# Second expert layer of a fused two-layer kernel on one Trainium2 core: factors of eight tiles at once, roots on VectorE, gathers before scatters, four and two banks

## What is computed

```python
gates = softmax(hn @ router_w.T)             # 8 experts, each token takes the best K = 2
h_e = gelu(hn @ w1[e]) @ w2[e]               # 128 -> 256 -> 128, for both experts e of a token
x = x + gate_1 * h_1 + gate_2 * h_2
...
mu = jnp.mean(x, axis=-1, keepdims=True)
out = (x - mu) * jax.lax.rsqrt(var + 1e-5)
```

## Time and profile before

| | |
|---|---|
| three runs, us | 2051.05, 2042.49, 2050.25 |
| median, us | 2050.25 |
| the profiled execution, us | 2048.84 |
| its span, us | 2046.8 |
| TensorE busy, us | 1752.1 (86%) |
| VectorE busy, us | 1418.8 (69%) |
| ScalarE busy, us | 1357.5 (66%) |
| GpSimd busy, us | 1056.0 (52%) |
| mean granted TensorE clock | 0.940 of full speed |

### The profile page before, as it was taken

The page is one execution under the profiler, slowest core; times in us unless marked ns, Lnnn a source line. Parts: engine busy times, 40 slices in busy tenths (PEclk is TensorE's granted clock), DMA queues, the critical chain, the costliest instruction groups (busy, mean ns, idle before and its releaser), DMA issues. The chain is left out here.

```text
span 2046.8 us, 52138 instructions
## 1 busy us (share of the span) xinstructions
PE 1752.1 (86%) x15928; PEld 1417.6 (69%) x15928; DVE 1418.8 (69%) x5901; ACT 1357.5 (66%) x3347; POOL 1056.0 (52%) x1384
## 2 busy tenths in 40 slices
PE   7789999999999998898999579888859999559885
PEld 6555555555555566787999458777738999529884
DVE  2378787878887885584432279999749889586775
ACT  3488888888888873423455358888749898417774
POOL 2133333333333323116567578888438899816664
PEclk9799999999999997999999779999979999859998
DMA  7789999999999973105576412222131222267552
GB/s 229 266 287 308 319 304 319 315 308 317 310 311 317 301 261 125 42 1 157 169 191 203 115 29 58 60 61 60 40 80 37 53 47 43 53 102 229 171 172 74
DMA packets 222093, 350.12 MB, mean 171 GB/s; under 512 B 56928, under 2 KB 169568, under 8 KB 221312
## 3 DMA queue, kind: packets, MB, share of 16 engines
q1 hardware_dynamic: 187024, 305.34, 47.6%
q0 software_dynamic: 14144, 31.16, 6.3%
q10 hardware_dynamic: 20656, 10.29, 1.7%
HBM read 160.82 MB, written 144.67 MB: 149 GB/s over the span
## 5 line engine op out<-in xcount | busy, mean ns | idle before, releaser
L183 POOL TENSOR_SCALAR_AFFINE_SELECT heads_raw_relative<-heads_raw_relative 128x508 f32<-128x508 f32 x256 | 166.7, 675 | 499.7 <-ACT heads_raw_relative L568 461.0
L568 ACT COPY heads_raw_relative<-heads_rel_bank 128x768 f32<-128x768 f32 x247 | 198.7, 804 | 125.1 <-PE heads_rel_bank L463 125.1
L492 PE MATMUL attend_turn_bank<-ident,attend_score 128*128 128x128 f32 x1536 | 232.8, 288 | 20.5 <-ACT attend_prob_t L574 19.2
L492 PEld LDWEIGHTS attend_turn_bank<-ident,attend_score 128*128 128x128 f32 x1536 | 164.3, 142 | 117.9 <-ACT attend_prob_t L574 68.3
L574 ACT ACTIVATE attend_prob_t<-attend_turn_bank 128x384 f32<-128x384 f32 x512 | 224.8, 500 | 7.3 <-PE attend_turn_bank L492 7.3
L578 ACT ACTIVATE attend_score<-attend_score,attend_extreme 128x128 f32<-128x128 f32 x512 | 215.6, 421 | 9.1 <-DVE attend_extreme L625 8.8
L625 DVE CUSTOM_DVE_ANT_0 attend_score<-attend_score_bank,heads_relative 128x256 f32<-128x256 f32 x512 | 215.0, 420 | 0.0
L622 DVE CUSTOM_DVE_ANT_0 attend_score<-attend_score_bank,heads_relative 128x128 f32<-128x128 f32 x512 | 146.7, 287 | 78.2 <-PE attend_score_bank L463 52.2
L631 DVE TENSOR_SCALAR attend_score<-attend_score,attend_extreme 128x256 f32<-128x256 f32 x512 | 195.7, 382 | 0.0
L1422 POOL DMA_INDIRECT moe_route_rows_sb<-tokens,moe_taken x154 | 145.7, 946 | 70.4 <-PE moe_route_bank L1444 42.0
L463 PE MATMUL attend_score_bank<-heads_qk 32*128 32x256 f32 x1024 | 156.9, 383 | 0.0
(11 more groups left out here) (434 smaller groups left out, 5257.5 us busy)
## 6 DMA issues: line engine op xcount, KB each, us to landing
shear<-heads_raw_relative SPq DMA_DIRECT2D x128, 768.0 KB, 5.4
heads_relative<-shear SPq DMA_DIRECT2D x128, 768.0 KB, 5.6
duo_w_now<-moe_w SPq DMA_DIRECT2D x158, 129.0 KB
moe_route_w_now<-moe_w SPq DMA_DIRECT2D x154, 129.0 KB
expert_out<-moe_route_y ACTq DMA_DIRECT2D x38, 256.0 KB
qk_heads<-heads_qk_out SPq DMA_DIRECT2D x32, 256.0 KB, 3.9
heads_qk<-qk_heads SPq DMA_DIRECT2D x128, 64.0 KB
pair_rows<-groups SPq DMA_DIRECT2D x16, 260.0 KB, 8.6
```

The lines of the kernel that those rows point to most:

```text
L183: m = nc.gpsimd.affine_select(out=future, in_=future, compare_op=ALU.is_ge, fill=-BIG, base=1 - P, pattern=[[0, QUAD], [1, P - 1]], channe ...
L492: mm = nc.tensor.transpose(bank[:, j * P:(j + 1) * P], score[:, (h - LAG) % RING, j * P:(j + 1) * P], c.ident[:, :])
L568: nc.scalar.copy(raw[:, ring, 2 * half:2 * half + 2, :], r_bank[:, :, 0:W]).then_inc(rel_moved, 1)
```

## The change

- GpSimd issues all 64 gathers and then all 64 scatters.
- The factors of eight tiles for all 32 steps of the walk are computed at once: `find_places(n)` for tiles 8n to 8n + 7 (seven operations, at u mod 16 = 4) and `weigh(n, lo, hi)` (five operations of up to 8 x 32 columns, at u mod 16 = 9, the third of which waits for the gathers of its tiles). `add_output` takes its factor from that table, by the register of the tile. The first eight tiles are done in two pieces: 0 and 1 at the start, 2 to 7 behind `add_output(0)`.
- The root goes to VectorE: eleven operations on up to 8 columns, each waiting for the one before (a first guess from the bits of the number and three Newton steps), in the place of the reciprocal. ScalarE keeps the copies and Gelu.
- The first product runs three units ahead, with four banks; the second has two banks, so `output(u)` waits for `add_output(u - 2)`.
- Registers are loaded for 8 units at a time (`UNITS_LOADED`), before for 4 (`LOADED`).

```diff
-    S, RING, DEEP, LEAD, AHEAD = UNITS, 12, 4, 36, 2
+    S, RING, DEEP, AHEAD, LOAD = UNITS, 12, 4, 3, UNITS_LOADED
+    HIDS, YS = 4, 2
+    PORTION, KEEP_AFTER = 8, 5
...
+        passed, stepped, of_low, weight = (c.rows[:, :, 32 * k:32 * (k + 1)] for k in range(4))
+        weight_from = D - NWALK
...
-            for t in range(NT + LEAD):
-                if t < NT:
-                    gather(t)
-                if t >= LEAD:
-                    scatter(t - LEAD)
+            for t in range(NT):
+                gather(t)
+            for t in range(NT):
...
-                wait_past(pe, hid_ready, u - 2)
+                wait_past(pe, hid_ready, u - HIDS + 1)
...
-                wait_past(pe, added, u - 2)
+                wait_past(pe, added, u - YS + 1)
...
-            def root(k):
-                cols = slice(starts[k], ends[k])
-                act.wait_ge(eps_set, 1)
-                act.wait_ge(moments_done, ends[k])
-                nc.scalar.activation(std[:, cols], moments[:, cols, 1], ACT.Sqrt, bias=eps[:, 0:1]).then_inc(rooted, 1)
-
...
+            def find_places(n):
+                cols = slice(PORTION * n, PORTION * (n + 1))
+                nc.vector.tensor_tensor(passed[:, cols, 0:NEDGE], bcast(pairs.slot_no[:, cols], NEDGE), along(pairs.until[:, :], PORTION),
+                                        ALU.is_ge).then_inc(placed, 1)
+                dve.wait_ge(placed, 7 * n + 1)
+                nc.vector.tensor_tensor(stepped[:, cols, 0:NEDGE], passed[:, cols, 0:NEDGE], along(pairs.step_code[:, :], PORTION), ALU.mult
...
-            def weigh(u, tile):
-                gathered(dve, needed(u))
-                dve.wait_ge(placed, 7)
-                wait_past(dve, shared_out, u - DEEP + 1)
-                nc.vector.scalar_tensor_tensor(out=part[u % DEEP][:, :], in0=flat(place[:, bass.ds(tile, 1), :]),
-                                               scalar=pairs.place_no[:, u:u + 1], in1=flat(rows_sb[:, bass.ds(tile, 1), 2 * D:]),
-                                               op0=ALU.is_equal, op1=ALU.mult).then_inc(parted, 1)
-
-            def share_of(u):
-                dve.wait_ge(parted, u + 1)
-                wait_past(dve, added, u - DEEP + 1)
-                nc.vector.tensor_tensor(share[u % DEEP][:, :], part[u % DEEP][:, 0:1], part[u % DEEP][:, 1:2], ALU.add).then_inc(shared_out, 1)
+            def weigh(n, lo, hi):
+                done, cols, count = 5 * n, slice(lo, hi), hi - lo
+                walk = along(pairs.unit_no[:, 0:NWALK], count)
+                dve.wait_ge(placed, 7 * ((hi - 1) // PORTION + 1))
+                nc.vector.tensor_tensor(of_low[:, cols, :], walk, bcast(place[:, cols, 0], NWALK), ALU.is_equal).then_inc(weighed, 1)
+                nc.vector.tensor_tensor(weight[:, cols, :], walk, bcast(place[:, cols, 1], NWALK), ALU.is_equal).then_inc(weighed, 1)
+                for t in range(lo, hi):
+                    gathered(dve, t)
+                dve.wait_ge(weighed, done + 1)
+                nc.vector.tensor_tensor(of_low[:, cols, :], of_low[:, cols, :], bcast(rows_sb[:, cols, 2 * D], NWALK), ALU.mult
...
+                nc.vector.tensor_tensor(weight[:, cols, :], weight[:, cols, :], of_low[:, cols, :], ALU.add).then_inc(weighed, 1)
 
             def add_output(u, tile):
                 dve.wait_ge(y_made, u + 1)
-                dve.wait_ge(shared_out, u + 1)
+                dve.wait_ge(weighed, 5 * sum(needed(u) >= first for first in weighed_from))
                 wait_past(dve, added, u)
                 total = flat(rows_sb[:, bass.ds(tile, 1), D:2 * D])
-                nc.vector.scalar_tensor_tensor(out=total, in0=y_bank[u % 3][:, 0:D], scalar=share[u % DEEP][:, 0:1], in1=total,
+                factors = weights_flat[:, weight_from + u:weight_from + u + (D - 2) * (NT - 1) + 1:D - 2]
+                nc.vector.scalar_tensor_tensor(out=total, in0=y_bank[u % YS][:, 0:D], scalar=factors[:, bass.ds(tile, 1)], in1=total,
                                                op0=ALU.mult, op1=ALU.add).then_inc(added, 1)
...
-            def invert(k):
-                cols = slice(starts[k], ends[k])
-                dve.wait_ge(rooted, k + 1)
-                nc.vector.reciprocal(rstd[:, cols], std[:, cols]).then_inc(inverted, 1)
+            def root(k):
+                cols, wide = slice(starts[k], ends[k]), slice(0, ends[k] - starts[k])
+                done = 11 * k
+                dve.wait_ge(moments_done, ends[k])
+                nc.vector.tensor_scalar(shifted[:, wide], moments[:, cols, 1], LN_EPS, None, ALU.add).then_inc(root_did, 1)
+                dve.wait_ge(root_did, done + 1)
+                nc.vector.tensor_scalar(rstd[:, cols].bitcast(I32), shifted[:, wide].bitcast(I32), -0.5, float(0x5f3759df), ALU.mult, ALU.add
+                                        ).then_inc(root_did, 1)
+                for i in range(3):
+                    dve.wait_ge(root_did, done + 3 * i + 2)
+                    nc.vector.scalar_tensor_tensor(out=step[:, wide], in0=rstd[:, cols], scalar=-0.5, in1=rstd[:, cols],
+                                                   op0=ALU.mult, op1=ALU.mult).then_inc(root_did, 1)
+                    dve.wait_ge(root_did, done + 3 * i + 3)
+                    nc.vector.tensor_tensor(step[:, wide], step[:, wide], shifted[:, wide], ALU.mult).then_inc(root_did, 1)
+                    dve.wait_ge(root_did, done + 3 * i + 4)
+                    nc.vector.scalar_tensor_tensor(out=rstd[:, cols], in0=step[:, wide], scalar=1.5, in1=rstd[:, cols],
+                                                   op0=ALU.add, op1=ALU.mult).then_inc(root_did, 1)
...
+            weighed_from = [0, 2] + list(range(PORTION, NT, PORTION))
...
+                    keep_at.setdefault(min(finished(end - 1) + KEEP_AFTER + j, S + 1), []).append((t, k))
+            find_places(0)
+            weigh(0, 0, 2)
+            for u in range(S + 2):
                 if u < S:
-                    if u + 1 < S:
-                        share_of(u + 1)
-                    add_output(u, tiles[u // LOADED % 2][u % LOADED])
+                    if u % LOAD == 0:
+                        tiles = tiles_of(mybir.EngineType.DVE, u)
+                    add_output(u, tiles[u % LOAD])
+                if u == 0:
+                    weigh(1, 2, PORTION)
+                following = u // 16 + 1
+                if u % 16 == 4 and following < NT // PORTION:
+                    find_places(following)
+                if u % 16 == 9 and following < NT // PORTION:
+                    weigh(following + 1, PORTION * following, PORTION * (following + 1))
```

106 lines of the change are left out of this document (45 added, 61 removed).

## The result

| | before | after |
|---|---|---|
| median of four runs, us | 2048.45 | 2071.36 |
| lowest and highest, us | 2042.49, 2051.05 | 2065.01, 2074.03 |
| profiled execution, its span, us | 2048.84, 2046.8 | 2069.09, 2067.3 |
| mean granted clock | 0.940 | 0.947 |

The ratio is 1.0104, with a 95% interval of 1.008 to 1.0127: the change makes the kernel 23 us slower. The forecast was 2047 us, 2028 to 2060. The time lies above the range, on the side to which I gave 0.14, and by none of the mechanisms that I listed for it.

What follows compares the result with a forecast made beforehand. TensorE was taken to bound the first 48 units or so, later ones losing time to ScalarE's table loads. Terms -8.5 (periods), +3.0 (before unit 50), +1.9 (end), +1.6 (clock) sum to -2.0 from 2048.84: 2047 us, range 2028 to 2060.

Steps and rivals of the forecast that it cites:

- the side to which I gave 0.14: Whole kernel: slower than before by over 0.5%, at a chance of 0.14.
- The tail from unit 146: End of the run: the keep of tile 48 comes behind a root of 2.1 us, not a 0.17 us reciprocal: +1.9 us.
- the stall changed its owner: Burst periods: TensorE's stall moves from ScalarE to VectorE at about its old size, 19.0 against 19.15 us; chance 0.53.
- one fall of the clock: TensorE, idling in pieces of 1.0 to 1.7 us, drops to half clock once: +1.6 us, bounds 0 and 13.
- a slack of 0.8 us: Second product with two banks: add_output u-2 may be 0.8 us late; a heavy half makes TensorE 3.8 us late.
- The six bursts ahead of unit 50: Finds and weighs at units 4, 9, 20, 25, 36 and 41 each hold the adds: +3.8 us.
- Registers are now loaded once in 8 units: VectorE's factor work: L2012 had waited 16.5 us for 40 register loads, 0.41 us each.
- Two units without keep are less still, about 1.0.: VectorE's work for two units without keep takes about 1.0 us, against TensorE's 1.89 us.
- The light half: The eight of 16 units without keeps, root or bursts; TensorE is the bound there, so no lateness is made good.
- The first (bursts cost half): VectorE's bursts cost about half of what was counted, through overlap or light units: 2033 us, faster, chance 0.33.
- The second (the clock falls with every burst): TensorE's clock halves at every burst, 8 to 11 times 1.7 us: 2061 us, slower, chance 0.14.
- no gap under 2 us does: Ground against the clock falling with bursts: in the earlier trace no TensorE gap under 2 us preceded a fall.

Runs made afterwards that it cites:

- the shorter portion: The spread kernel with three banks and loads of four, its portion of tiles 48 to 55 cut in two: 2021.8 us (0.9891).
- the spread kernels: Changed kernel, find, weigh and first six roots issued one or two operations behind each add_output: 2021.7 us (three banks, loads of four), 2040.9 us (change's banks and loads).

## Why the prediction was wrong

**What held.** Durations: the root spans 2.27 us (2.1), the find from 1913.18 to the operation behind it 2.15 (2.1), the weigh 1.8 (1.9). ScalarE's table waits left TensorE. Gathers ahead cost nothing. The tail from unit 146 grew by 2.4 us (+1.9), and the root makes most of it: back on ScalarE it leaves 32.0 us. By the shorter portion the scatters are not alone in that tail, though. The sense of the mechanism held as well: the stall changed its owner, and the second product waits for add_output at three places in each burst period.

**How much each missing piece is worth.** The traces of the spread kernels part the miss. The first column is the forecast less what it gave to bursts; the others are measured from add_output to add_output, each in one execution:

| units, us | forecast without bursts | spread, three banks, loads of four | spread, banks and loads of the change | the change | forecast |
|---|---|---|---|---|---|
| 0 to 50 | 49.5 | 49.4 | 55.5 | 61.1 | 53.3 |
| 50 to 114 | 60.4 | 61.4 | 69.7 | 89.0 | 76.0 |
| 114 to 146 | 30.2 | 29.3 | 33.4 | 35.1 | 30.4 |
| all | 140.1 | 140.1 | 158.7 | 185.2 | 159.7 |

The first two columns agree, within 1.0 us in each line, so the work itself was sized right. Two banks with loads of eight add 18.6 us where no burst stands, and the forecast had nothing for them. The bursts add 26.5 us where it had 19.6, and 1.6 apart for one fall of the clock, which lies within the 26.5. So the larger failure is the term that is absent; the slack is the smaller one.

**The step that came first in the argument and failed: "a slack of 0.8 us".** I took three blocks of 0.45 us less a product's tail of 0.16 and the add's 0.35. In the trace after, the add_output starts 0.88 us behind its product's start (1908.24 to 1909.12) where I had 0.45 + 0.16, and the waiting product starts some 0.26 us behind the add's end (1912.43 to 1912.69), where I had nothing. From product to product that is 0.88 + 0.35 + 0.26 = 1.49 us, of 1.89 that two units of TensorE take: a slack of 0.4. The first of these stood in the trace of before: the restart at 1899.46 and its add_output at 1900.32 are 0.86 us apart. By the rows above the root then makes TensorE 1.67 us late and the find 1.62 (due at 1913.79 + 0.89 = 1914.68, started at 1916.30); with 1.1 for the weigh that is 4.4, and I had 3.8 us for the bursts of a period. (The six bursts ahead of unit 50 I also added up wrongly: 3 x 0.7 + 2 x 0.5 + 1 is 4.1 us, not 3.8.) In the last two periods I gave a root next to nothing, and the two there cost 1.7 us. What spreading gives at the change's banks and loads is 2069.3 - 2040.9 = 28.4 us, over the ten periods or parts of them.

**The term that is absent: register loads on TensorE.** "Registers are now loaded once in 8 units" was counted as a saving on VectorE only. On TensorE a load of eight takes 0.7 us at the median. Of the period behind unit 50, 21.8 us, 15.1 are products, 4.4 the lateness by root, find and weigh (1.67 and 1.62 as above, 1.1 for the weigh), and 2.1 the places at three of its loads.

With the bursts spread, loads of eight against four cost 8.3 us with two banks by the medians (5 by the ratios); with three banks the medians differ by 2.7 us, which the intervals do not tell from nothing, and the two traces from unit 0 to 146 by 6.1 (146.2 and 140.1). How far a third bank covers loads of eight thus stays open. The third bank gives 16.5 us with loads of eight and 10.9 with four, the latter on one chip.

The place of the loss is clear. With bursts spread and the change's banks and loads, the second products of units 2 to 146 come 21.8 us later in all than TensorE's pace, and 19.2 of that at the 36 units that stand just behind a load of TensorE (u mod 8 is 0 or 5); with loads of four it is 12.4 of 13.4 us, at 72 such units. At every second of the 36 places VectorE loads its tiles too, and no run parts the two engines' loads.

In the early units, which TensorE had filled before, the bursts are 5.6 us (61.1 - 55.5) where I had 3.8, as the wait for the rows of tiles 2 to 7 is in both kernels; the 6.1 us of banks and loads (55.5 - 49.4) were not in my sum. Why two banks uncover a load I read from its place: a sequencer that stands at a wait for add_output until just before the product can run reaches the load late. That is argued from starts, and no run changed it by itself.

**"Two units without keep are less still, about 1.0."** The light half was to be VectorE's time to recover. In the changed kernel two add_outputs never start less than 0.7 us apart, so it can make good only 0.2 us a unit, not 0.4. What that costs no run shows by itself. With three banks a burst period still takes 19.9 us: the second products of units 6, 8, 13 and 14 of 16 come 0.7, 1.6, 1.2 and 0.7 us behind TensorE's pace on average.

**Rivals.** The first (bursts cost half) is wrong by its sign. The second (the clock falls with every burst) is wrong too: at the root and find shown above TensorE idles 0.78 and 1.46 us, and the clock stays full. But the ground that I gave against it was misread. I had "no gap under 2 us does", and the gap of the earlier trace rows, which a fall follows, is 1.93 us. In the changed kernel the clock falls once, behind an idle time of 1.55 us that ends at 1938.08:

```profile
1938.08 0.71 PE L1935 MATMUL duo_y_bank<-moe_w,duo_hid 128*128 x4 [1.55 <-DVE duo_rows_sb L2025]
...
1940.00:1942.00 2.00, 2.00 (x12) 2.00 (x11) 0.61 (x3) 0.63 (x2) 1.61 (x2) 0.50 0.14 45
1942.00:1944.00 2.00, 2.00 (x14) 2.00 (x14) 0.96 (x4) 1.14 (x4) 1.48 (x2) 0.65 0.41 134
```

A second trace of the same kernel has two such falls, each behind 1.55 us and each 1.7 us lost. That is one or two in ten portions, as I had taken one. I had named the Trainium skill (TensorE: Matmul & The Clock Gate, A second HAM failure mode: psum-queue depth-cycling) for this rival; a clock that swings to and fro throughout, as that section describes it for another kernel, these traces do not show. What I lacked on the slower side was the case that held: a stretch that TensorE had filled, and that the change opens with waits of its own.

**The sum.** Against the forecast the start and the first 50 units are 5.8 us worse (10.8 - 2.0 where I had 3.0), the six periods 17.7 (124.1 where I had 106.4), the end 0.5, and the 1.6 us for the clock, which I had put apart, came as the one fall within the 89.0: 5.8 + 17.7 + 0.5 - 1.6 = 22.4 us, the miss between the profiled spans (20.5 + 2.0 = 22.5).

## What to carry to other kernels

Count a bank's slack from start to start of the waiting instructions, with the hand-over on both sides, in rows of the trace; the arithmetic of busy times gave twice what there was. Before you take a bank away, list all that it hides: here it hid not only VectorE's delays but TensorE's own register loads. Work that an in-order engine does once in 16 units belongs in the gaps between the instructions that others wait for, one or two operations at a time: with three banks and loads of four that turned the loss of 23 us into a gain of 20 to 23 us, with the same operations. And a register load is a cost on each engine that does it, to be looked for in the rows of the engine that is the bound.
